# A graph network on one core: dense stages in three steps instead of two, and a bias product of 512 columns

## The reference

```
h = relu(layernorm(x)); x = x + L0(h, ...)   # two relational convolutions, 10 relations
h = relu(layernorm(x)); x = x + L1(h, ...)   # one, 3 relations, then relu
h = relu(layernorm(x)); x = x + L2(h, ...)   # two SAGE convolutions, a norm over nodes, h @ fcW.T + fcb
h = relu(layernorm(x)); x = x + L3(h, ...)   # filtered messages, then ssp(agg @ W_out1 + b_out1) @ W_out2 + b_out2
```

## Time and profile before

| | |
|---|---|
| median of three runs | 16276.06 us |
| the profiled execution | 16305.06 us, span 16303.3 us |
| busy share of the span | POOL 66%, PE 51%, DVE 42%, PEld 41%, ACT 19% |
| chain that ended last, by engine | POOL 53%, issue 22%, DMA 11%, PE 7%, DVE 4%, ACT 2% |
| chain, lines of the dense stages | PE L1040 2%, PE L998 1%, PE L997 1%, PE L1028 1%, PE L1035 1% |
| granted clock of PE, mean | 0.593 of full speed |

### The profile page before, as it was taken

One profiled execution on the slowest core, in us unless ns is written; L12 is line 12 of the kernel. 1 busy time (PEld: TensorE's weight loads), 2 busy tenths in 40 slices (PEclk: granted clock), 3 DMA queues, 4 the chain that ended last, 5 costly groups with the idle time before them and its releaser, 6 DMA issues.

```text
span 16303.3 us, 178889 instructions
## 1 busy us (share of the span) xinstructions
PE 8334.2 (51%) x36107; PEld 6626.3 (41%) x36108; DVE 6832.8 (42%) x28429; ACT 3056.0 (19%) x6469; POOL 10804.4 (66%) x10307
## 2 busy tenths in 40 slices
PE   2374444474444444444534444444444777777777
PEld 1144444433333333333433333333333655555555
DVE  7642222245555433333333333355554344444443
ACT  0043223220000010000200000100000444444443
POOL 0027777737777657777477777577775488888882
PEclk6585555585555565555655555555555677777775
DMA  3053334341211231211211111333333466666665
GB/s 98 9 205 105 105 104 104 100 169 52 52 52 52 73 88 52 52 52 52 71 51 52 52 52 52 83 103 103 103 103 82 94 117 118 118 118 118 118 119 122
DMA packets 1043046, 1437.00 MB, mean 88 GB/s; under 512 B 208285, under 2 KB 644148, under 8 KB 1042956
## 3 DMA queue, kind: packets, MB, share of 16 engines
q0 software_dynamic: 552016, 851.84, 24.2%
q1 hardware_dynamic: 490984, 584.65, 12.3%
HBM read 1101.27 MB, written 334.40 MB: 88 GB/s over the span
## 4 chain that ended last, share of the span: by engine, by line
POOL 53%; issue 22%; DMA 11%; PE 7%; DVE 4%; ACT 2%; POOLq 1%; DVEq 1%; ACTq 0%; SPq 0%
POOL scratch L647 35%; POOL rows L647 13%; DMA agg_dram<-acc,sum_row 9%; POOL agg_dram L629 5%; PE ps L1040 2%; PE ps L998 1%; DVE tab_s L1187 1%; DMA table_dram<-tab_s 1%; PE ps L997 1%; PE ps L852 1%; PE ps L1035 1%; PE ps L1028 1%; ACT xn_h L784 0%; DMA acc<-in_attr 0%; DVE scratch L1155 0%
## 5 line engine op out<-in xcount | busy, mean ns | idle before, releaser
L647 POOL DMA_INDIRECT scratch<-table_dram,row_st x5936 | 5679.9, 957 | 1809.9 <-issue 1809.6
L869 PE MATMUL ps<-scratch 128*128 128x128 f32 x7776 | 1971.4, 434 | 2845.3 <-DMA scratch<-table_dram,row_st 2788.4
L1201 DVE TENSOR_TENSOR acc<-ps,acc 128x128 f32 x2080 | 607.3, 292 | 6053.5 <-PE ps L869 5848.2
L629 POOL DMA_INDIRECT agg_dram<-acc,sum_row x1664 | 2642.5, 1588 | 529.3 <-issue 389.3
L869 PEld LDWEIGHTS ps<-scratch 128*128 128x128 f32 x7776 | 1710.0, 324 | 3103.3 <-issue 1973.4
L647 POOL DMA_INDIRECT rows<-table_dram,row_st x2384 | 2279.2, 956 | 789.4 <-issue 746.6
L869 PE MATMUL ps<-tab_s,rows 128*128 128x128 f32 x4224 | 1060.2, 431 | 1565.1 <-DMA rows<-table_dram,row_st 1510.4
L869 PE MATMUL ps<-tab_s,scratch 128*128 128x128 f32 x4096 | 1050.1, 438 | 1516.8 <-DMA scratch<-table_dram,row_st 1445.3
L702 ACT ACTIVATE row_st<-row_i 128x16 int32 (+1 forms) x520 | 111.1, 215 | 8998.2 <-PE ps L869 8952.5
L869 PEld LDWEIGHTS ps<-tab_s,rows 128*128 128x128 f32 x4224 | 919.2, 321 | 1703.1 <-issue 1032.0
L869 PEld LDWEIGHTS ps<-tab_s,scratch 128*128 128x128 f32 x4096 | 911.9, 328 | 1654.0 <-issue 996.7
(11 more groups left out here) (197 smaller groups left out, 12324.6 us busy)
## 6 DMA issues: line engine op xcount, KB each, us to landing
scratch<-in_src_row SPq DMA_DIRECT2D x832, 256.0 KB
table_dram<-tab_s POOLq DMA_DIRECT2D x200, 640.0 KB, 3.2
scratch<-type_dram SPq DMA_DIRECT2D x416, 256.0 KB, 3.4
scratch<-in_dst_row SPq DMA_DIRECT2D x416, 256.0 KB
scratch<-table_dram,row_st POOLq DMA_INDIRECT x5936, 2.5
rows<-table_dram,row_st POOLq DMA_INDIRECT x2384, 2.5
scratch<-table_dram SPq DMA_DIRECT2D x416, 64.0 KB
agg_dram<-acc,sum_row POOLq DMA_INDIRECT x1664, 4.0
```

What stands on the lines that cost most here:

```text
L629: pool.indirect_dma_start(agg_dram[j], bass.IndirectOffsetOnAxis(ap=sum_row[:, QUAD * q + j:QUAD * q + j + 1], axis=0), sums[:, q, j * P:( ...
L647: pool.indirect_dma_start(row_tile(bank, u), None, table_dram[p["rels"]], bass.IndirectOffsetOnAxis(ap=row_st[:, bank, u:u + 1], axis=0)). ...
L869: mm = pe.matmul(ps[bank][:, q * P:(q + 1) * P], row_tile(row_bank, u), hot[:, u, :], start=u % QUAD == 0, stop=u % QUAD == QUAD - 1)
L1201: dve.tensor_tensor(window, ps[bank][:, q * P:(q + 1) * P], window, ALU.add).then_inc(add_done, 1)
```

## The change

Two edits. First, in stages k = 2, 3 and 5 a body gets a third superblock, `ahead` = f + 1: ACT reads its sums into yT behind the square root of f, and PE does its update between the transposition and the products of l. The loop's first update and first x step have bodies of their own, and so have the last two bodies. Second, `update` in the stages with a bias row (k = 5 and 6) forms one bias product of 512 columns from a row written four times (`row_quad`, eight small DVE copies at the start) instead of four of 128 columns; the four weight products then accumulate on it.

```diff
+            if has_upd(p):
+                body(None, None, ahead=0)
+                if nsb > 1:
+                    body(0, None, ahead=1)
...
+                if nsb > 2:
+                    with e.Fori(0, nsb - 2) as i:
+                        body(i + 1, i, ahead=i + 2)
+                if nsb > 1:
+                    body(nsb - 1, nsb - 2)
+                body(None, nsb - 1)
+                return
...
@@ scalar
+                    if ahead is not None and p["src"] != "sum":
+                        to_update(ahead)
                     if l is not None and has_root(p):
...
@@ tensor
                 def update(i):
                     pe.wait_ge(x_new, i + (turns(k, has_x) + 1))
+                    if "row" in p:
+                        pe.matmul(ps[0][:], ones[0:1, :], row_quad[p["row"]][:], start=True, stop=False)
                     for j in range(4):
-                        o = ps[0][:, j * P:(j + 1) * P]
-                        if "row" in p:
-                            pe.matmul(o, ones[0:1, :], bias_row[p["row"]][:], start=True, stop=False)
-                        mm = pe.matmul(o, yT[:, j * P:(j + 1) * P], W[p["upd"]][:], start="row" not in p, stop=True)
+                        mm = pe.matmul(ps[0][:, j * P:(j + 1) * P], yT[:, j * P:(j + 1) * P], W[p["upd"]][:],
+                                       start="row" not in p, stop="row" not in p or j == 3)
...
-                    if f is not None and has_upd(p):
-                        pe.wait_ge(y_ready, f + (turns(k, has_src) + 1))
-                        update(f)
...
                         mm.then_inc(hT_mm, 1)
+                        if ahead is not None:
+                            pe.wait_ge(y_ready, ahead + (turns(k, has_src) + 1))
+                            update(ahead)
                         pe.wait_ge(hT_ready, l + (n + 2))
...
@@ vector, at the start
+            for n in row_quad:
+                for j in range(4):
+                    step(dve.tensor_copy(row_quad[n][:, j * P:(j + 1) * P], bias_row[n][:]))
```

More of the change, by code:

```diff
@@ L153, in build @@
         bias_row = {n: sb(n, [1, P]) for n in ROWS}
+        row_quad = {n: sb(f"{n}_quad", [1, BANK]) for n in ("fcb", "bout2")}
         bfilt2_quad = sb("bfilt2_quad", [3 * PART, BANK], BF16)
@@ L390, in superblocks @@
                     body(i, i)
+                return
[3 more added lines that the diff above has]
+                    body(0, None, ahead=1)
+                else:
+                    body(0, None)
+                if nsb > 2:
[4 more added lines that the diff above has]
+                body(None, nsb - 1)
                 return
@@ L741, in _, with body, to_update @@
                     nc.scalar.preload_act_table_set("natural_log_exp_and_others")
[L743 to L749, removed]
+                def body(f, l, b=0, uses=0, ahead=None):
+                    def to_update(y):
+                        acc_y = acc[:, bass.ds(y * SB, SB)]
+                        if has_upd(p):
+                            act.wait_ge(upd_mm, y + turns(k, has_upd))
+                        else:
+                            act.wait_ge(tab_mm, y * nck + (chunks(k) + 1))
                         settle(act)
                         if p["src"] == "copy":
-                            act.activation(yT[:], acc_f, ACT.Copy).then_inc(y_ready, 1)
+                            act.activation(yT[:], acc_y, ACT.Copy).then_inc(y_ready, 1)
                         elif p["src"] == "relu":
-                            act.activation(yT[:], acc_f, ACT.Relu).then_inc(y_ready, 1)
+                            act.activation(yT[:], acc_y, ACT.Relu).then_inc(y_ready, 1)
                         elif p["src"] == "bn":
-                            act.activation(yT[:], acc_f, ACT.Identity, bias=bn[:, 6:7], scale=bn[:, 5:6]).then_inc(y_ready, 1)
+                            act.activation(yT[:], acc_y, ACT.Identity, bias=bn[:, 6:7], scale=bn[:, 5:6]).then_inc(y_ready, 1)
+                    if f is not None:
+                        if has_src(p) and not has_upd(p):
+                            to_update(f)
                         elif p["src"] == "sum":
@@ L993, in update, with body @@
                     pe.wait_ge(x_new, i + (turns(k, has_x) + 1))
+                    if "row" in p:
+                        pe.matmul(ps[0][:], ones[0:1, :], row_quad[p["row"]][:], start=True, stop=False)
                     for j in range(4):
-                        o = ps[0][:, j * P:(j + 1) * P]
-                        if "row" in p:
-                            pe.matmul(o, ones[0:1, :], bias_row[p["row"]][:], start=True, stop=False)
-                        mm = pe.matmul(o, yT[:, j * P:(j + 1) * P], W[p["upd"]][:], start="row" not in p, stop=True)
+                        mm = pe.matmul(ps[0][:, j * P:(j + 1) * P], yT[:, j * P:(j + 1) * P], W[p["upd"]][:],
+                                       start="row" not in p, stop="row" not in p or j == 3)
                     mm.then_inc(upd_mm, 1)
-                def body(f, l, b=0, uses=0):
+                def body(f, l, b=0, uses=0, ahead=None):
                     if p["src"] == "sum":
```

## The result

The changed kernel takes 16230.74 us (median of eight runs, 16225.66 to 16234.08), the kernel before 16276.29 us (eight runs). The ratio is 0.9972 with a 95% interval of 0.9961 to 0.9983: 0.28% faster, 46 us, where 63 were forecast. The profiled execution has a span of 16224.4 us, 79 less than before.

What follows compares the result with a forecast made beforehand. POOL's gathers, untouched, hold most of the span; in the dense stages PE's update is on the path. Terms 25 + 8 + 2 - 54 - 44 = -63 us take 16305.06 to 16242, by the median 16213 us; range 16160 to 16255.

Steps and rivals of the forecast that it cites:

- a clock that never rises in k = 5 and 6: Rival: these stages gain only 42 and 38 us, the rest loses 35; 16231 us, chance 0.12.
- The bias product: PE's update in k = 5 and 6: six fewer weight changes at 0.25 us save 1.5 us a superblock.
- The rival that it gives nothing: Merged bias product saves nothing in k = 6, k = 5 gains a few us; about 16305 us, chance 0.06.
- k = 6: Only the bias product changes: 1.75 us a superblock over 25, 44 us gained (bounds 38 and 60).
- The floor by the load of the old x: In k = 6, load issued 3.7 us after the x step and taking 4.8 limits the period to 8.6 us.
- k = 5: Period 11.73 to 10.1 us at 1.2 GHz, taken as 9.6 with partial clock rise: 54 us gained.
- k = 2: Period 7.19 to 7.76 us at full clock, taken as 8.4 with clock falls after PE's pause: 25 us lost.
- the store of the table: Must land before the next copies into `tab_s`, which come over 4 us later; counted as nothing.
- k = 3: Period 8.39 to about 8.85 us, between 7.86 at full clock and 10.0 at half: 8 us lost.
- Start: Eight added DVE copies at the kernel's start, where DVE is on the path: 2 us lost.
- The slower end: PE's pause before the update takes the full clock from k = 2 and 3: 16331 us, chance 0.06.
- The clock that rises for good in k = 5 and 6: Longer PE runs raise the clock, gaining 111 and 60 us instead of 54 and 44: 16140 us, chance 0.12.

Runs made afterwards that it cites:

- the kernels with full rows: Bias product given 128 zero-padded rows: on the kernel before, 16152.73 us; merged, on the changed kernel with ACT reading the next sums at the body's head, 16001.50 us.
- the faster kernels: Changed kernel with the update behind the table products on PE, 16052.41 us; or with ACT reading the next sums at the body's head, 16017.80 us.
- the bias-only kernel: Kernel before with only the bias product merged to 512 columns and the eight copies, two-step order kept: 16197.22 us, ratio 0.9948.
- the full-row kernel: Kernel before with its four bias products of 128 columns given weights of 128 rows, zero but for row 0: 16152.73 us, ratio 0.9925.

## Why the prediction was right, and where its sizes were off

**The direction and the mechanism.** The two edits pull against each other as forecast: k = 2 and 3 lose, k = 5 and 6 gain by the bias product. The two experiments with one edit each show it. In k = 5 the new order gives little; the worked 10.1 us at 1.2 GHz is the measured 10.04. The gains of k = 5 and 6 come to 97 us, where 98 were forecast, but this is luck in part: k = 5 gave less than its term and k = 6 more. What is missing from the 63 us is in the losses, 45 us with the start instead of 35. That makes 52 us in the stages, against 46 between the medians. That the measured time is the 16231 us priced for a clock that never rises in k = 5 and 6 is a coincidence: the clock did rise there, and both gains and losses are larger than in that rival.

**The bias product.** Mis-sized: 1.5 us forecast, 1.78 measured. The change of weights costs 0.29 us, not 0.25: the pair without a change was put at 0.47 us, from a run of passes with the start and the tail in it, and is 0.43. The rival that it gives nothing is refuted.

**k = 6.** 44 us forecast, 45.8 measured between the x steps, near 48 with the first update. Many periods are 9.21 us, which is 10.99 less 1.78; short rises of the clock to 0.59 on average make the mean 9.08. This lies under the 9.3 to 9.6 us that the prediction gave as a sign, and the update took 4.1 us from its start to the x step, not 4.4. The floor by the load of the old x was put at 8.6 us (its terms, 3.72 and 4.8, give 8.5); the kernels with full rows stand on it at 8.64, where the x step waits for that load in 22 superblocks.

**k = 5.** 54 us forecast; 47.7 between the x steps and about 2 in the first update. Here the term that was mis-sized is the rise of the clock. The first period (7.43 us) gained 4.1 us against 3.5 forecast; the 23 others were taken at 9.6 us and are 9.83 on average, which is 5 us over the stage. The clock did rise, but the rows show where: in most superblocks at the end of the run of passes, in the transposition, which is off the path, and then while PE waits. In a few superblocks the rise reached the path, with periods down to 8.96 us.

**k = 2.** 25 us forecast, 30.3 measured. The period at full clock was worked out as 7.76 and is 7.71; the pause as 3.0 and is 3.08. The fall of the clock was put in half of the superblocks at 1 to 1.5 us; it comes in half of them and costs 9.41 - 7.71 = 1.7 us, so the 23 later periods are 8.60 us on average and not 8.4. One step was wrong and did no harm: the store of the table was counted as nothing because the next copy comes over 4 us later. In the superblocks at full clock the first copies do wait for it, DVE's 10 times and 29.8 us in all, but the last copy still waits for PE there:

```profile
5718.24 0.56 DVE L1450 COPY tab_s<-ps 128x384 f32<-128x384 f32 x1 [2.89 <-DMA table_dram<-tab_s]
...
5719.44 0.56 DVE L1450 COPY tab_s<-ps 128x384 f32<-128x384 f32 x1 [0.64 <-PE ps L1064]
```

In the faster kernels this store is the bound of the stage.

**k = 3.** 8 us forecast, 12.4 measured. The 23 later periods, taken at 8.85, are 9.07 us on average. At full clock the period is 7.87 us where 7.86 was worked out, so the mechanism held, and the term that was mis-sized is the mixture. Between 7.86 and 10.0 us a clock of 0.74 gives 8.97 and not 8.85; the clock of the stage was 0.78. The forecast loss is also a difference against an average that is itself a mixture: with the same code in this stage, before has 8.39, the bias-only kernel 8.15 and the full-row kernel 7.99. Against these two the loss would be 18 and 22 us, so its size is open by some 10 us.

**Start.** The eight copies take twice 0.96 us on DVE, and DVE's work behind them starts 2.0 us later than before, as forecast. In the total it cannot be seen: the first x step of k = 2 came 2.9 us earlier than before, with the edge passes in between varying by more.

**The rivals.** The slower end (the clock lost for good in k = 2) did not come: behind update, tables and transposition without a break the clock is back within one superblock. The clock that rises for good in k = 5 and 6 did not come either, and the kernels with full rows show the reason that the prediction had only guessed: with them k = 6 went from 0.59 to 0.81, and k = 5, once it also read the sums first, to 0.98.

## What to carry to other kernels

When a stage is given one more step of lookahead, ask for each engine what now stands between the new early work and the old critical one: here the update was early, but it waited for ACT, and the table products and the x step waited behind it. Moving one ACT instruction to the head of the body turned a loss of 43 us in two stages into a gain of 75. A bias by a one-row product is cheap in columns and dear in two other ways, the change of weights and the clock; a zero-padded row with full weights took no more time here, removed the first and most of the second, for a tile of 128 rows instead of one. When a stage gets faster, order its loads by who needs them first.

## What was not expected of the hardware

- A change between one-row and full weights cost 0.29 us at 1.2 GHz, shown as idle time of 0.22 to 0.23 us in front of the weight load; between full weights there is none.
- PE's clock stood at 0.50 with PE busy 81% and 87% of the time, where half of the passes of the update had one row. The same count of passes with full rows brought it to 0.75 and 0.81 in the same order of work.
- The granted clock was 1.00 in a stretch of 2 us in which PE only waited, and 0.50 in the work that followed (k = 5 after).
- The load of the old x took 4.7 us behind four loads of the partial sums and 3.0 us ahead of them.
